# A four-block transformer kernel on one core: where the first attention's weighted sums stand in TensorE's instruction order

## What is computed

```python
x = x + _L0_attn_ref(_layernorm(x, axis=-1), L0_attn_Wq, ..., L0_attn_proj)
...
q = jnp.einsum('bse,hde->bhsd', x, Wq) + bq[None, :, None, :]
k = jnp.einsum('bse,hde->bhsd', x, Wk) + bk[None, :, None, :]
v = jnp.einsum('bse,hde->bhsd', x, Wv) + bv[None, :, None, :]
causal = jnp.triu(jnp.ones((s, s), bool), 1)
scores = jnp.einsum('bhsd,bhtd->bhst', q, k) / scale
scores = jnp.where(causal[None, None], -jnp.inf, scores)
att = jax.nn.softmax(scores, axis=-1) / scale
z = jnp.einsum('bhst,bhtd->bhsd', att, v)
z = z.reshape(b, s, h * dh)
return z @ proj
```

## Time and profile before

| | |
|---|---|
| Time, median of 3 runs | 1301.98 us (1298.15 to 1303.81) |
| The profiled execution's own time | 1300.24 us |
| Its span in the trace | 1298.5 us |
| PE busy | 1161.7 us, 89% |
| DVE busy | 855.1 us, 66% |
| ACT busy | 708.2 us, 55% |
| POOL busy | 540.7 us, 42% |
| Mean granted TensorE clock | 0.942 of 2.4 GHz |

### The profile page before, as it was taken

One profiled execution on the slowest core, in us unless ns is written; L12 is line 12 of the kernel. 1 busy time (PEld: TensorE's weight loads), 2 busy tenths in 40 slices (PEclk: granted clock), 3 DMA queues, 4 the chain that ended last, 5 costly groups with the idle time before them and its releaser, 6 DMA issues.

```text
span 1298.5 us, 17287 instructions
## 1 busy us (share of the span) xinstructions
PE 1161.7 (89%) x5970; PEld 638.7 (49%) x5970; DVE 855.1 (66%) x1624; ACT 708.2 (55%) x941; POOL 540.7 (42%) x445
## 2 busy tenths in 40 slices
PE   4799999999999999999856689999999959999998
PEld 2455545555545555545434423333333326787876
DVE  5576776776776686776543515554343557999999
ACT  3354455454455444445312178888888838566664
POOL 1356565556565555565610000000000013787876
PEclk9799999999999999999965789999999978999999
DMA  3110111111111111111200000000000000221210
GB/s 106 24 39 23 33 39 31 32 39 31 25 39 31 31 40 31 31 33 30 52 1 0 1 3 1 1 3 1 2 0 1 1 1 1 100 82 65 75 54 33
DMA packets 25924, 37.80 MB, mean 29 GB/s; under 512 B 11444, under 2 KB 14148, under 8 KB 24828
## 3 DMA queue, kind: packets, MB, share of 16 engines
q1 hardware_dynamic: 25852, 36.87, 10.9%
HBM read 18.96 MB, written 1.11 MB: 15 GB/s over the span
## 4 chain that ended last, share of the span: by engine, by line
PE 54%; DVE 28%; issue 10%; ACT 5%; POOL 1%; DMA 1%; DVEq 0%; SPq 0%; ACTq 0%
PE banks L901 8%; PE banks L892 6%; PE banks L378 6%; PE banks L323 6%; PE banks L304 5%; DVE qb L1171 5%; DVE mxa L542 4%; PE banks L363 4%; PE banks L364 3%; DVE banks L547 3%; PE banks L397 3%; ACT prob L910 2%; PE banks L387 2%; DVE kb L527 2%; DVE zz L577 2%
## 5 line engine op out<-in xcount | busy, mean ns | idle before, releaser
L656 POOL TENSOR_TENSOR pacc<-pacc,prob 128x1024 f32<-128x1024 f32 (+3 forms) x160 | 274.5, 1716 | 72.9 <-ACT prob L468 63.4
L910 ACT ACTIVATE prob<-banks 128x1024 f32<-128x1024 f32 x256 | 249.3, 1025 | 55.9 <-PE banks L892 55.9
L468 ACT ACTIVATE prob<-banks 128x1024 f32<-128x1024 f32 x192 | 155.9, 812 | 194.4 <-PE banks L364 193.5
L1204 POOL TENSOR_TENSOR ka<-prob,qb 128x512 fp32r<-128x512 f32 x108 | 165.1, 1550 | 60.1 <-ACT qb L1154 33.3
L378 PE MATMUL banks<-prob,v 128*64 128x512 f32 (+3 forms) x768 | 166.4, 512 | 1.6 <-POOL prob L647 1.6
L363 PE MATMUL banks<-qa,ka 128*128 128x512 f32 (+3 forms) x384 | 157.4, 418 | 2.0 <-ACT prob L468 1.3
L858 POOL TENSOR_TENSOR sq<-sq 64x512 f32<-64x512 f32 x8 | 8.3, 1035 | 334.3 <-DVE sq L854 334.3
L323 PE MATMUL banks<-ka,qa 128*128 128x512 f32 (+3 forms) x384 | 110.1, 398 | 39.6 <-DVE mxa L542 32.4
L901 PE MATMUL banks<-prob,v 128*32 128x512 f32 x1024 | 138.1, 612 | 0.6 <-ACT prob L910 0.6
L647 POOL TENSOR_SCALAR_AFFINE_SELECT prob<-prob 128x256 f32<-128x256 f32 x128 | 52.2, 408 | 197.7 <-ACT prob L468 197.6
L1160 ACT ACTIVATE prob<-banks,w 128x512 f32<-128x512 f32 x144 | 94.5, 686 | 70.9 <-PE banks L1122 70.7
(11 more groups left out here) (192 smaller groups left out, 1754.8 us busy)
## 6 DMA issues: line engine op xcount, KB each, us to landing
qb<-qa SPq DMA_DIRECT2D x64, 128.0 KB, 2.3
ka<-ka SPq DMA_DIRECT2D x64, 128.0 KB, 2.3
prob<-gate_rows SPq DMA_DIRECT2D x8, 1024.0 KB, 4.8
w<-in_experts SPq DMA_DIRECT2D x9, 514.0 KB, 3.5
wqkv<-in_wqkv SPq DMA_DIRECT2D x16, 193.0 KB, 2.4
x<-in_x SPq DMA_DIRECT2D x4, 256.0 KB, 3.9
out<-x SPq DMA_DIRECT2D x4, 256.0 KB, 2.2
wpr<-in_wpr SPq DMA_DIRECT2D x1, 512.0 KB, 6.0
```

The costliest lines, as they stand in the source:

```text
L468: act.activation(pr[:, j % NRING, :, 0:wd], banks[:, 0:2, 0:wd], ACT.Exp, scale=SCALE0).then_inc(s_exp, 1)
L656: pool.tensor_tensor(pacc[:, sbk, :, o:BLK], pacc[:, sbk, :, o:BLK], pr[:, j % NRING, :, 0:wd], ALU.add).then_inc(s_padd, 1)
L910: act.activation(prob[:, j % NP1, :], banks[:, 2 * (j % 2):2 * (j % 2) + 2, :].rearrange("p b c -> p (b c)"), ACT.Exp, scale=2 * SCALE1).t ...
L1204: pool.tensor_tensor(act2[1][:, tb % 2, i, :], hid[:, tb % 2, i, :], act2[0][:, tb % 2, i, :], ALU.subtract).then_inc(s_hlP, 1)
```

## The change

For every even slot j the weighted sum that stood behind `scores_pe(j)` is moved behind `scores_pe(j + 1)`, directly in front of the one that stands there. So slot 1 has those of slots 10 and 11 of the unit before, slot 3 those of 0 and 1, slot 5 of 2 and 3, slot 7 of 4 and 5, slot 9 of 6 and 7, slot 11 of 8 and 9. No instruction is added or removed, and the lists of ACT, DVE, POOL and SP stay as they are.

```diff
@@ -429,9 +429,11 @@
                         qk_pe(pe, n, x_, bn, 1, False)
                 elif j == 2:
                     turn_pe(pe, u, 1, first)
-                if j < 2 and not first:
-                    pv_pe(pe, u - 1, x_, j + 10, first)
-                elif j >= 2:
+                if j == 1 and not first:
+                    pv_pe(pe, u - 1, x_, 10, first)
+                    pv_pe(pe, u - 1, x_, 11, first)
+                elif j > 1 and j % 2:
+                    pv_pe(pe, u, w, j - 3, first)
                     pv_pe(pe, u, w, j - 2, first)
                 if j == 2 and not first:
                     sums_pe(pe, u - 1, 1, False)
```

## The result

The changed kernel takes 1307.16 us (median of 20 runs, 1300.95 to 1314.03); in the same measurement the kernel before takes 1301.0 us (20 runs, 1291.05 to 1304.13). The ratio, which is that of the two means, is 1.0055, with a 95% interval of 1.0037 to 1.0074: 7 us slower (the medians are 6.2 us apart). I had forecast 17 to 18 us slower; the measured time lies just inside the stated range, 1306 to 1328 us. The profiled execution has a span of 1301.4 us and a time of 1303.23 us, so this trace is one of the faster ones of its kernel.

The account below looks back on a forecast made before the run. PE has most work but runs into DVE in each unit, the chain changing hands four times. 0.86 + 0.66 - 0.35 = 1.17 us a unit gave 16.9 us in all, 1319 us timed (1.3% slower), range 1306 to 1328 us.

Parts of the forecast that it names:

- Slots 7 to 9, +0.86 us: Slots 7 to 9: projection still waits for `yneg`, displaced sum follows the scores of slot 9, fourth maxima step 0.86 us later.
- the two values for the projection's 1.12 us: Slot 8: loss of 0.86 us if the 1.12 us contains only the wait, 0.60 us if also a change of split.
- Slots 1 to 5, +0.66 us: Slots 1 to 5: displaced sums and a bare wait for slot 4's exponential make the output projection 0.66 us later.
- Slots 5 to 7, -0.35 us: Slots 5 to 7: paired sums save 0.15 us, the second maxima step not following a weighted sum 0.20 us.
- the walk: Following the chain through one unit: 0.8 to 1.4 us more a unit, 1313 to 1323 us; chance 0.62.
- I take no change: Lower-clock stretches in the attention's units: their number stays at seven, each costing 0.96 us.
- one for the worse (0.18): Rival "Walk and clock": added idleness brings the lower clock in nearly every unit, 1327 us or a little more; chance 0.18.
- none of the seven: Attention's units: no stretch at the lower clock left would be a gain of 6.7 us.
- its wait would stay near 2 us: Slot 11, a sign to look for on the timeline after: PE's wait there still near 2 us.
- First and last unit: First unit 0.5 us longer (0.86 - 0.35), having no unit before it; last unit left at 0.
- The two cancel: Rival: slot 5's wait shorter, slot 8's projection containing the change of split; 0.25 us a unit, 1306 us; chance 0.12.
- The saved changes of split decide: Rival: all five saved pairs on the path, 15 x 1.75 = 26 us off, 1276 us; chance 0.08.

Follow-up runs that it names:

- slot 8 alone: Kernel before with only the weighted sum of slot 8 moved, behind the scores of slot 9: 1316.3 us, ratio 1.0131.
- Slot 0 alone: Kernel before with only the sum of slot 10 of the unit before moved, from slot 0 to slot 1: 1303.88 us, ratio 1.0029.
- slot 2 alone: Kernel before with only the weighted sum of slot 2 moved, behind the scores of slot 3: 1293.98 us, ratio 0.9961.
- slot 6 alone: Kernel before with only the weighted sum of slot 6 moved, behind the scores of slot 7: 1286.77 us, ratio 0.9904.
- Slot 10 alone: Kernel before with only the weighted sum of slot 10 moved, behind the scores of slot 11: 1291.78 us, ratio 0.9937.
- all but slot 10: Changed kernel with the sum of slot 10 back in its old place: 1316.15 us, ratio 1.0132 to the kernel before.
- slot 4 alone: Kernel before with only the weighted sum of slot 4 moved, behind the scores of slot 5: 1301.72 us, ratio 0.9991.
- all but slot 8: Changed kernel with the sum of slot 8 back in its old place: 1295.62 us, ratio 0.9960 to the kernel before.

## Why the prediction was off

The direction and the place of the losses were right; the size was not, 7 us instead of 17. The largest part of the difference is the clock, which the sum took as unchanged and which gave back 5 us between the traces; the next is a term of 3.5 us that the sum lacked in slots 5 to 7. Point by point:

- **Slots 7 to 9, +0.86 us: right.** 0.82 us in the chain, 0.86 by slot 8 alone, 0.86 by taking it back. Of the two values for the projection's 1.12 us the one that I took is right: it takes 1.12 us behind the wait with no weighted sum ahead of it.
- **Slots 1 to 5, +0.66 us: right in size (0.64), by luck in part.** Two errors cancel. The first maxima step waits for the copy of k, which I had not on my list: the second k part on ACT stands behind the exponential of slot 2, I had seen that it comes 0.4 us later, and did not follow it through SP's copy to `max_pe`. This makes the scores of slot 5 0.2 us later than the exponential would. They then take 1.01 and not 1.21 us, since they do not stand behind a bare wait. Slot 0 alone gave 0.43 of the 0.45 us, and slot 2 alone 0.25 us of gain by the way over ACT which I had dismissed.
- **Slots 5 to 7, -0.35 us: right for the pairs (0.37 by slot 6 alone), but a term is missing.** The output projection takes 1.95 us where it follows a pair of weighted sums directly, and 2.20 us where PE had waited for z before it. It is no change of split, since a weighted sum, of half width too, stands in front of it in both kernels. It is what a matmul group pays behind a wait: the projection of two passes takes 0.86 us directly behind a maxima step (at 338.20) and 1.12 us behind the wait for `yneg`, 0.26 us more, and that is the same with a weighted sum in front of the wait and with scores in front of it (384.57). I had the two values before me and used them for the projection of slot 8 alone. With this term the walk gives 0.92 us a unit, and 0.87 is measured: 14 x 0.25 = 3.5 us of the 10 that were too many.
- **The clock, "I take no change": wrong.** This is the step that failed: the term was put at nothing, and the only change of the clock with a chance of its own was one for the worse (0.18), though "none of the seven" stood beside it as a gain of 6.7 us, and a rarer lower clock among the signs of being wrong. I argued that PE would be idle longer and at more places. In sum it was, and the lower clock came less often all the same, once in these units and not seven times. What I said of slot 11, that its wait would stay near 2 us, was wrong: the fifth maxima step now comes before DVE has finished the fourth, so the wait falls into two (0.73 and 1.33 us), and the lower clock no longer follows it. Slot 10 alone (nothing moved on the path, seven stretches gone, 0.6% faster) and all but slot 10 (same path as the change, eight stretches, 1.3% slower) show it from both sides. Between the traces of before and after it is worth 5 us (7.76 against 2.80 us), between all but slot 10 and the change 9 us by the medians and 10 us by the ratios, 6.7 us of which can be counted in the units. With the clock not given back, all but slot 10 is 1.3% slower, which is what the sum had forecast for the whole change. The price of a stretch, 0.96 us, was too low as well: the 13 units from 137.56 us take in the last one, of 36.96 us, and counted from the first projection (99.59 to 600.96 us) it is 7.76 / 7 = 1.11 us.
- **First and last unit.** The first output projection comes 0.69 us earlier than before, where I had 0.5 us later; a stretch of lower clock at 81 us is missing in front of it; the last unit's end is 1.1 us shorter, because its sums (line 387) take 1.10 us at full clock and took 2.00 us at half. Both are the clock again, in these two traces.
- **Behind the attention** the changed kernel's trace is 2.2 us shorter (633.9 against 636.1 us from the last output projection on). Nothing is changed there, and over the twelve other traces this part lies between 631.6 and 640.9 us: it is the scatter of single executions, and single spans should not be compared to a few us.
- **The rivals.** "The two cancel" was the nearest in time, but not by its reasons: slots 1 to 5 and the projection of slot 8 cost what the walk had for them, and what cancelled was the clock. "The saved changes of split decide" is wrong for the set as a whole, and right for slot 6, where PE is the bound. The Trainium skill's rule that a change of the tiling mode drains TensorE (TensorEngine Tiling, Key Properties) agrees with the 0.35 us a pair, by slot 6 alone 0.37; it says nothing of whether PE is waited for.

That cutting the idle place keeps the clock up does not rest on one pair of kernels: in the six traces with 1.33 us (units of 37.4 to 38.8 us) none of 84 such places is followed by the lower clock, in the eight with 1.9 or 2.1 us (units of 37.6 to 38.9 us) 46 of 112 are. But with the place at 1.9 us their number differs: seven in both traces of before and in slot 4 alone, two in slot 6 and in slot 2 alone, five in slot 0 alone.

The times at which the stretches begin show more of it. In before these are 235.3, 272.8, 351.3, 388.9, 467.4, 504.9 and 583.4 us, so 37.5 or 78.5 us apart, although the units between them are of 37.97 and 39.1 us; the two of slot 6 alone and the two of slot 2 alone stand 37.5 us apart too. The stretches keep a pace of their own, not that of the units, and an idle place of 1.9 us meets one at some moments and not at others (the one at 311.99 us does not, that at 349.94 us does, with the same instructions around them). How often the places come at such a moment goes by how far the unit's length is from that pace: with units of 37.60 us the places stay for many units at a moment that is spared (mean clock 0.950 over six executions), with 37.72 us less surely (0.945), with 37.97 us they do not (0.941). So an estimated 5 of the 12 us of slot 6 alone (five stretches fewer at 1.1 us) are luck in the unit's length, which a further change can take away again. This is read off the traces; no run changed the length of the unit alone.

That the packet of the instruction queue makes single copies of k late stays open, and so does what starts it.

## What to carry to other kernels

Before a filler is moved off a place, ask what wait it lies under: a weighted sum that fills the wait for another engine costs nothing where it is, and its full time where it goes; grouping such work saves its changes of split only where PE itself is the bound, so move the one that qualifies (slot 6 here) and not all six. Follow the delay of every producer through copies on the DMA queues too. And when the order around a wait changes, work out whether the idle place stays in one piece, since that decided here whether the lower clock could come at all, and the sum of idle time did not; how often it comes to a long one depends on the unit's length, so a gain or loss of 0.5% in a loop like this one can be the clock alone.

## What the runs showed of the hardware

- In the attention's units (90 to 640 us) of the 14 traces there are 48 stretches of some 3 us at the lower clock, 1.2 GHz, and each begins between 0.3 us before and 1.6 us behind the end of an idle place of PE of 1.85 to 2.2 us: 46 in slot 11, two behind a late copy of k. Of the 112 places of 1.9 or 2.1 us in slot 11, 46 had one; of the 84 of 1.33 us none had, nor had the one of 1.73 us (all but slot 8, behind a late copy), nor those of 0.5, 0.73, 0.84 and 1.03 us. The changed kernel has five places of 0.5 to 1.33 us in each unit, with PE's busy time from 100 to 640 us at 474 us where before has 507. The Trainium skill, TensorE: Matmul & The Clock Gate, Part 1, says that the throttled state is the default and that activity releases it; the runs agree in that each of the 48 stretches stands beside idleness of PE.
- A stretch at the lower clock cost a unit 1.1 to 1.2 us where it began in slot 11 (39.11 against 37.97 us in before, 38.80 against 37.60 in slot 6 alone). The unit of the changed kernel in which it began in slot 4 is 2.6 us longer, of which 1.35 us is the longer wait for the copy (1.85 against 0.50 us).
- A group of matmuls behind a wait takes about 0.25 us longer than directly behind other matmuls: 1.12 against 0.86 us for a projection of two passes, 2.20 against 1.95 us for an output projection.
- Two weighted sums one after the other take 1.87 us with 512 columns, against 2 x 1.01 apart, and the scores behind them pay 0.20 us once and not twice.
